# State update and r times h of a gated graph network in whole instructions of 1,024 columns instead of two halves of 512

## The reference, cut to what matters

```
m = adj @ h                                   # in_matrix = out_matrix = adj
z = sigmoid(m @ (w3a + w3b).T + b3 + h @ u3.T + c3)
r = sigmoid(m @ (w4a + w4b).T + b4 + h @ u3.T + c3)
v = tanh(m @ (w5a + w5b).T + b5 + (r * h) @ u5.T + c5)
h = (1 - z) * h + z * v
```

## Time and profile before

| | us |
|---|---|
| median of 3 runs | 1640.51 (1640.27 to 1640.82) |
| the profiled execution | 1640.93 |
| its span, first to last instruction | 1639.1 |

### The profile page before, as it was taken

One profiled execution on the slowest core, in us unless ns is written; L12 is line 12 of the kernel. 1 busy time (PEld: TensorE's weight loads), 2 busy tenths in 40 slices (PEclk: granted clock), 3 DMA queues, 4 the chain that ended last, 5 costly groups with the idle time before them and its releaser, 6 DMA issues.

```text
span 1639.1 us, 23869 instructions
## 1 busy us (share of the span) xinstructions
PE 1561.4 (95%) x7471; PEld 720.4 (44%) x7471; DVE 1217.6 (74%) x2142; ACT 752.5 (46%) x1154; POOL 369.6 (23%) x801
## 2 busy tenths in 40 slices
PE   5699999999999999999999999999999999999997
PEld 4344444444444444444444444444444444444443
DVE  6587777877688776877678877787777876777677
ACT  3155443545444454354544455345553545445554
POOL 4335003430125202170021700236003340030000
PEclk8799999999999999999999999999999999999998
DMA  3121112211121111211113111221112211121111
GB/s 145 26 52 26 33 32 68 48 33 31 38 64 45 32 29 35 72 43 29 35 32 83 26 38 26 49 69 35 26 38 64 51 26 38 38 49 29 38 26 52
DMA packets 214229, 71.75 MB, mean 44 GB/s; under 512 B 208192, under 2 KB 209088, under 8 KB 214208
## 3 DMA queue, kind: packets, MB, share of 16 engines
q1 hardware_dynamic: 212480, 70.83, 18.5%
q10 hardware_dynamic: 1728, 0.66, 0.2%
HBM read 13.24 MB, written 8.39 MB: 13 GB/s over the span
## 4 chain that ended last, share of the span: by engine, by line
PE 56%; DVE 22%; issue 9%; ACT 8%; DMA 2%; SPq 1%; POOL 1%; DVEq 0%; ACTq 0%; POOLq 0%
PE ps_m L562 33%; DVE z L1065 3%; DVE cand L957 3%; PE ps_u L584 3%; PE ps_u L585 3%; PE ps_u L583 3%; PE ps_v L584 3%; PE ps_v L585 3%; PE ps_v L583 3%; PE ps_r L583 2%; PE ps_r L585 2%; PE ps_r L584 2%; ACT z L814 2%; DVE cand L949 2%; DVE h_lo L968 2%
## 5 line engine op out<-in xcount | busy, mean ns | idle before, releaser
L562 PE MATMUL ps_m<-adj_hi,nh_hi 128*128 128x512 f16 x1280 | 485.3, 379 | 17.2 <-ACT m_hi L748 13.4
L562 PE MATMUL ps_m<-adj_lo,nh_hi 128*128 128x512 f16 x1280 | 485.3, 379 | 0.0
L562 PE MATMUL ps_m<-adj_hi,nh_lo 128*128 128x512 f16 x1280 | 485.2, 379 | 0.0
L949 DVE SCALAR_TENSOR_TENSOR cand<-cand,h 128x512 f32<-128x512 f32 x160 | 139.6, 894 | 135.4 <-ACT cand L760 135.4
L748 ACT ACTIVATE m_hi<-ps_m 128x512 f16<-128x512 f32 x192 | 110.7, 588 | 276.6 <-PE ps_m L562 275.8
L743 ACT ACTIVATE h_hi<-h 128x512 f16<-128x512 f32 x158 | 97.3, 630 | 245.4 <-DVE h L961 245.4
L940 DVE SCALAR_TENSOR_TENSOR m_lo<-ps_m,m_hi 128x512 f16<-128x512 f32 x192 | 129.2, 685 | 97.6 <-ACT m_hi L748 97.6
L562 PEld LDWEIGHTS ps_m<-adj_hi,nh_hi 128*128 128x128 f16 x1280 | 125.3, 98 | 172.0 <-ACT m_hi L748 12.5
L1046 DVE SCALAR_TENSOR_TENSOR rh<-ps_r,w_inv,hu 128x512 f32<-128x512 f32 x160 | 120.0, 750 | 102.9 <-PE ps_r L585 100.0
L562 PEld LDWEIGHTS ps_m<-adj_hi,nh_lo 128*128 128x128 f16 x1280 | 125.3, 98 | 151.2 <-issue 0.3
L562 PEld LDWEIGHTS ps_m<-adj_lo,nh_hi 128*128 128x128 f16 x1280 | 125.3, 98 | 147.4
(11 more groups left out here) (144 smaller groups left out, 2424.3 us busy)
## 6 DMA issues: line engine op xcount, KB each, us to landing
x_in<-in_x_dram SPq DMA_DIRECT2D x16, 512.0 KB, 3.3
out_dram<-y SPq DMA_DIRECT2D x16, 512.0 KB, 2.7
adj_in<-in_adj_dram SPq DMA_DIRECT2D x8, 512.0 KB, 7.4
nh_hi<-h_hi SPq DMA_TRANSPOSE x128, 2.4
nh_lo<-h_lo SPq DMA_TRANSPOSE x128, 2.4
h_hi<-nh_hi SPq DMA_TRANSPOSE x32, 2.4
h_lo<-nh_lo SPq DMA_TRANSPOSE x32, 2.4
n_hi<-h_hi SPq DMA_TRANSPOSE x30, 2.4
```

Source lines behind the costliest of these rows:

```text
L562: last = nc.tensor.matmul(ps_m[half][:, :], a[slot][:, k, :], b[:, k, cols(half)], start=(k == 0 and n == 0), stop=(k == BLOCKS - 1 and n ...
L949: nc.vector.scalar_tensor_tensor(out=cand[:, c], in0=cand[:, c], scalar=SCALE16, in1=h[slot][:, c], op0=ALU.mult, op1=ALU.subtract).then_i ...
```

## The change

The two halves of six operations become one instruction over all 1,024 columns, each after a wait for both halves of its source: `h_hi` and `rh_hi` on ScalarE, and on VectorE the difference, the product with z, the sum into h, `h_lo`, r times h and `rh_lo`. Each adds 2 to its semaphore, so that counts for the others stay as they were. The sums from PSUM, the tanh, the sigmoid of r and `m_hi`, `m_lo` stay in halves.

```diff
             def round_h(q, slot):
-                for half in range(2):
-                    act.wait_ge(h_ready, 2 * q + half + 1)
-                    nc.scalar.activation(h16_hi[slot][:, cols(half)], h[slot][:, cols(half)], ACT.Copy
-                                         ).then_inc(h16_hi_done, 1)
+                act.wait_ge(h_ready, 2 * q + 2)
+                nc.scalar.activation(h16_hi[slot][:, :], h[slot][:, :], ACT.Copy).then_inc(h16_hi_done, 2)
...
-                for half in range(2):
-                    c = cols(half)
-                    act.wait_ge(rh_done, 2 * q + half + 1)
-                    nc.scalar.activation(rh_hi[:, c], rh[:, c], ACT.Copy).then_inc(rh_hi_done, 1)
+                act.wait_ge(rh_done, 2 * q + 2)
+                nc.scalar.activation(rh_hi[:, :], rh[:, :], ACT.Copy).then_inc(rh_hi_done, 2)
...
             def new_state_begin(slot, q):
-                for half in range(2):
-                    c = cols(half)
-                    dve.wait_ge(cand_ready, 2 * q + half + 1)
-                    nc.vector.scalar_tensor_tensor(out=cand[:, c], in0=cand[:, c], scalar=SCALE16, in1=h[slot][:, c],
-                                                   op0=ALU.mult, op1=ALU.subtract).then_inc(diff_done, 1)
+                dve.wait_ge(cand_ready, 2 * q + 2)
+                nc.vector.scalar_tensor_tensor(out=cand[:, :], in0=cand[:, :], scalar=SCALE16, in1=h[slot][:, :],
+                                               op0=ALU.mult, op1=ALU.subtract).then_inc(diff_done, 2)
             def new_state_end(slot, q):
                 dve.wait_ge(z_ready, q + 1)
-                for half in range(2):
-                    c = cols(half)
-                    dve.wait_ge(diff_done, 2 * q + half + 1)
-                    nc.vector.tensor_mul(cand[:, c], cand[:, c], z[slot][:, c]).then_inc(zdiff_done, 1)
-                for half in range(2):
-                    c = cols(half)
-                    dve.wait_ge(zdiff_done, 2 * q + half + 1)
-                    nc.vector.tensor_add(h[slot][:, c], h[slot][:, c], cand[:, c]).then_inc(h_ready, 1)
+                dve.wait_ge(diff_done, 2 * q + 2)
+                nc.vector.tensor_mul(cand[:, :], cand[:, :], z[slot][:, :]).then_inc(zdiff_done, 2)
+                dve.wait_ge(zdiff_done, 2 * q + 2)
+                nc.vector.tensor_add(h[slot][:, :], h[slot][:, :], cand[:, :]).then_inc(h_ready, 2)
             def rest_h16(slot, q):
...
+                dve.wait_ge(h16_hi_done, 2 * q + 2)
+                nc.vector.tensor_sub(h16_lo[slot][:, :], h[slot][:, :], h16_hi[slot][:, :]).then_inc(h16_lo_done, 2)
...
+                dve.wait_ge(r_ready, 2 * q + 2)
+                nc.vector.tensor_mul(rh[:, :], rh[:, :], h[slot][:, :]).then_inc(rh_done, 2)
+                dve.wait_ge(rh_hi_done, 2 * q + 2)
+                nc.vector.tensor_sub(rh_lo[:, :], rh[:, :], rh_hi[:, :]).then_inc(rh_lo_done, 2)
```

More of the change, by code:

```diff
@@ L944, in new_state_begin @@
             def new_state_begin(slot, q):
-                for half in range(2):
-                    c = cols(half)
-                    dve.wait_ge(cand_ready, 2 * q + half + 1)
-                    nc.vector.scalar_tensor_tensor(out=cand[:, c], in0=cand[:, c], scalar=SCALE16, in1=h[slot][:, c],
-                                                   op0=ALU.mult, op1=ALU.subtract).then_inc(diff_done, 1)
+                dve.wait_ge(cand_ready, 2 * q + 2)
+                nc.vector.scalar_tensor_tensor(out=cand[:, :], in0=cand[:, :], scalar=SCALE16, in1=h[slot][:, :],
+                                               op0=ALU.mult, op1=ALU.subtract).then_inc(diff_done, 2)
             def new_state_end(slot, q):
                 dve.wait_ge(z_ready, q + 1)
-                for half in range(2):
-                    c = cols(half)
-                    dve.wait_ge(diff_done, 2 * q + half + 1)
-                    nc.vector.tensor_mul(cand[:, c], cand[:, c], z[slot][:, c]).then_inc(zdiff_done, 1)
-                for half in range(2):
-                    c = cols(half)
-                    dve.wait_ge(zdiff_done, 2 * q + half + 1)
-                    nc.vector.tensor_add(h[slot][:, c], h[slot][:, c], cand[:, c]).then_inc(h_ready, 1)
-            def rest_h16(slot, q):
[L965 to L969, removed]
+                dve.wait_ge(diff_done, 2 * q + 2)
+                nc.vector.tensor_mul(cand[:, :], cand[:, :], z[slot][:, :]).then_inc(zdiff_done, 2)
+                dve.wait_ge(zdiff_done, 2 * q + 2)
+                nc.vector.tensor_add(h[slot][:, :], h[slot][:, :], cand[:, :]).then_inc(h_ready, 2)
+            def rest_h16(slot, q):
+                dve.wait_ge(h16_hi_done, 2 * q + 2)
+                nc.vector.tensor_sub(h16_lo[slot][:, :], h[slot][:, :], h16_hi[slot][:, :]).then_inc(h16_lo_done, 2)
             def output(n, slot, pairs):
```

## The result

The changed kernel takes 1865.68 us (median of 4 runs, 1864.54 to 1866.92) against 1640.66 of the kernel before (4 runs, 1640.27 to 1641.11) on the same chip: ratio 1.137, 95% interval 1.136 to 1.139. Slower was right, 1794 us was not: 225 us were lost, 154 forecast, and the time lies outside 1762 to 1835.

What follows compares the result with a forecast made beforehand. TensorE was taken as the bound. Ordinary rounds (36 x 1.81 = 65.2), layer rounds (36.7) and the other rounds sum to 153.7 us on 1640.93, forecasting 1794 us at chance 0.80, range 1762 to 1835.

Steps and rivals of the forecast that it cites:

- An instruction that waits for the one before starts 0.03 us after its end: Gap assumed for waits within and between engines, 0.03 us, read from the trace of the kernel before.
- GpSimd isn't moved as much, they miss each other and the round becomes an ordinary one: Two rounds where GpSimd's L438 meets the difference, 7 each: 1.81 less today's wait of 0.22 and 0.63, 19.4 us.
- Rival 1: TensorE's clock falls to 1.2 GHz in the layer rounds' waits: 14 times 1.5 us lost, 1816 us; chance 0.09.
- the layer rounds: Both layer rounds of a pair, 14 in all: chain already ends last, shift 2.62 each, 36.7 us; waits about 2.3.
- The 0.07 a pair on VectorE: Saving from merging two VectorE halves: 1.22 us whole against 1.28 to 1.30 for halves, 0.07 us a pair.
- The 0.16: Saving of a VectorE pair by the skill page's formula alone, 0.16 us, by which the change would look a gain.
- The first wait alone: TensorE before finish_candidate, waiting for rh_lo: matmul at 951.66 instead of 950.66, 1.00 us in every round having one.
- The second: TensorE before the r product, waiting for m_lo, 3.05 us later: 0.81 us more, 1.81 with the first wait.
- 31, 13 and 22 us: Upper ends of unknown terms: VectorE at 1.29, some 31; ScalarE at 1.15, 13; GpSimd meeting the chain as today, 22.
- Rival 2: Only the wait at finish_candidate counts, idle time absorbs the second: 77 rounds x 1.00, 1718 us; chance 0.08.
- Rival 3: Not slower: cover at both waits exceeds lost overlap, saved overhead gains about 16 us, 1625 us; chance 0.03.
- price 0: The four transposes start about 3.0 us later but stay hidden, keeping over 1 us before the next big product.

Runs made afterwards that it cites:

- counts of one: Changed kernel with plain DMA copies for the transposes, each whole instruction adding 1 to its semaphore instead of 2: 1804.74 us against 1868.37.
- the form with copies: DMA transposes replaced by plain DMA copies of the same tiles, h not turned: kernel before 1622.12 us, changed kernel 1868.37 us.
- the state update alone: Kernel before with plain copies, only difference, product with z, sum into h, h_hi and h_lo made whole: 1721.77 us, +99.7 over its base.

## Why the prediction was wrong

The mechanism stood, and so did where it acts: two waits on one chain, the first for `rh_lo`, the second for `m_lo` of half 0 behind the z chain. What failed is the size of one term, and with it two clauses on what else moves.

- **"An instruction that waits for the one before starts 0.03 us after its end"**: this is the step that failed. It was read from instructions that carry a count of one, and the eight whole ones of a round carry a count of two; they start 0.10 after. With them the ordinary round came out at 19.27 instead of 18.65. With counts of one it is 18.76, and the forecast's arithmetic meets it within 0.11. Over the kernel this is some 41 of the 71 us missed, worked out from the rounds that meet nothing else.
- **"GpSimd isn't moved as much, they miss each other and the round becomes an ordinary one"**: true of the difference in both rounds, but `rh_lo` of the second moved into GpSimd's instruction. 19.4 forecast, 40.8 measured. That round is 21.18 without a fall of the clock, and an ordinary one 19.27, so the meeting costs 13 us here; in the form with copies, cutting GpSimd's instruction gives back 16.6 in that round. The 19.4 has a slip, too: it takes off the idle times of 0.22 and 0.63 of the brackets, but the delays are 0.38 and 0.78 (17.22 and 17.62 against 16.84), so its own arithmetic gives 17.2.
- **Rival 1, the clock, given 0.09, came in part.** I had the waits of the layer rounds at 2.3; they became 2.98 to 3.23. The late starts are about 0.4 of it: with counts of one they are 2.57 and 2.82, and the clock falls there as well. It costs some 8 us in all: 4.8 in the row of the table, about 2 in the first step of slot 0 and 1.3 in the round that meets GpSimd. The price of a fall was about right (up to 1.7 for 1.5), the number of rounds that pay it too high. The Trainium skill, page "TensorE: Matmul & The Clock Gate", section "HAM oscillation — how this bites in real kernels", puts the idle time that matters above every one in the loop of the changed kernel. The traces don't agree: the clock fell after 2.88 to 3.23 us here, and after 2.56 with counts of one. It was wrong to hold the rival down by that rule.
- Durations: 1.23 and 1.06 measured, 1.22 and 1.06 forecast. The 0.07 a pair on VectorE is right. The formula of the Trainium skill, page "VectorE: DVE Perf Modes", section "The TRN2 errata — SBUF-src ops pay a fixed extra latency per instruction", gives an estimate of 1.22 us for one instruction of 1,024 columns, and the trace agrees with its 1.22 to 1.23. The 0.16 that the prediction worked out from it for a pair the trace doesn't show: two halves back to back take 1.28 to 1.30, not twice 0.69.
- The first wait alone: 1.00 forecast, 1.21 measured (three late starts at 0.07 each). The second: 0.81 against 1.23 (five more, 0.35 of the 0.42). These are delays; the idle times that the prediction named as its signs are 0.16 less, 1.05 and 1.07 in the trace.
- The range was narrower than its own terms: 31, 13 and 22 us above 1794 make 1860, not 1832, and no term stood for a start later than 0.03.
- Rival 2, only the first wait counts, is refuted by the state update alone, which has no first wait and loses 99.7 us. Its observation was sound, though: VectorE's idle time while `rh_hi` is made could be used, by an order that puts the sum for z in it, and then the second wait is gone.
- Rival 3, saved overhead decides, is refuted: VectorE's busy time fell by 52 us and the time rose.
- The transposes: "price 0" holds in ordinary rounds. In the first step of a pair the kernel before depends on them, as the 18 us between its two forms show; its rows point at those of the output and of the first h, not at those that bring h for the big product.

The 71 us missed, by parts: 41 the count, 13 GpSimd, 8 the clock. Of the rest, some 9 us, about 4 are the 0.11 in each of 36 ordinary rounds and 5 the layer rounds, whose shift of 2.62 would still be too small with counts of one; other kinds came out a little below. Why, I haven't taken apart.

## What to carry to other kernels

Before merging two halves of a chain that alternates between engines, write down when each consumer starts with halves and with the whole, and compare the delay with the slack at every wait of the bound engine: a delay within it costs nothing (+0.11 for 1.3 us here), a delay beyond it is paid once a step, and slack can be spent once. Read the cost of a handoff from instructions that carry the same semaphore count. After a shift, look again at which instructions of GpSimd now lie beside which of VectorE, and which of the two starts first.

## What was not expected of the hardware

An instruction of VectorE or ScalarE whose semaphore count is two starts 0.07 us later than one with a count of one, at 128x8, 128x512 and 128x1024 alike and whatever its releaser counts (0.10 against 0.03). Where VectorE's `rh_lo`, with two operands in SBUF, and a GpSimd instruction over 1,024 columns meet, the one that starts second is held up: `rh_lo` takes 3.11 us instead of 1.23, or GpSimd 3.41 instead of 2.34. TensorE's clock fell to its lower level after idle times from 2.56 us on and stayed at its upper one after some of up to 3.43, so the idle time alone doesn't tell. A fall cost up to 1.7 us in the changed kernel.
